# Reordering the first attention layer of a two-layer attention and experts kernel: scores, values and bias in a new order on four engines

## What is computed

```python
x = x + window_attention(group_norm(x))   # layer 0: 8x8 windows, shifted by 4; 12 heads of 8; cosine scores
t = t + local_attention(layer_norm(t))    # layer 1: 6 heads of 16, causal, window of 16
t = t + experts(layer_norm(t))            # 4 experts, best 2, hidden 384
```

```python
qkv = xw @ qkv_w.T + qb                                   # xw: 64 windows of 64 tokens
qn = q / max(norm(q), 1e-12);  kn = k / max(norm(k), 1e-12)
attn = einsum('whid,whjd->whij', qn, kn) * scale + bias + mask
out = einsum('whij,whjd->whid', softmax(attn), v)
out = out @ proj_w.T + proj_b
```

## Time and profile before

| | |
|---|---|
| median of three runs | 470.01 us (470.0 to 472.74) |
| profiled execution | 472.79 us, its span 471.0 us |
| PE busy | 420.6 us (89%) |
| DVE busy | 337.6 us (72%) |
| ACT busy | 342.5 us (73%) |
| POOL busy | 125.2 us (27%) |
| layer 0, steps 0 to 31 | about 28 to 187 us of the span |

### The profile page before, as it was taken

The page is one execution under the profiler, slowest core; times in us unless marked ns, Lnnn a source line. Parts: engine busy times, 40 slices in busy tenths (PEclk is TensorE's granted clock), DMA queues, the critical chain, the costliest instruction groups (busy, mean ns, idle before and its releaser), DMA issues.

```text
span 471.0 us, 14649 instructions
## 1 busy us (share of the span) xinstructions
PE 420.6 (89%) x5292; PEld 318.7 (68%) x5292; DVE 337.6 (72%) x949; ACT 342.5 (73%) x918; POOL 125.2 (27%) x300
## 2 busy tenths in 40 slices
PE   4669999999999987799999998879999999999995
PEld 2436667676766666577777776658865777777773
DVE  4857878878787886667677667463669677777776
ACT  3457887878787873788888887654786777777773
POOL 5122233242424330433343433546502000000000
PEclk9999899999999999999999999876999999999999
DMA  7400000000000000000000000005000503302200
GB/s 206 121 2 1 2 2 0 0 0 0 0 0 0 0 3 1 2 3 2 0 0 0 0 0 3 2 1 135 1 2 22 150 1 83 86 1 83 83 17 17
DMA packets 7861, 12.17 MB, mean 26 GB/s; under 512 B 2179, under 2 KB 6681, under 8 KB 7062
## 3 DMA queue, kind: packets, MB, share of 16 engines
q1 hardware_dynamic: 7322, 11.60, 9.1%
q0 software_dynamic: 96, 0.09, 0.2%
q10 hardware_dynamic: 412, 0.08, 0.1%
HBM read 10.08 MB, written 1.68 MB: 25 GB/s over the span
## 4 chain that ended last, share of the span: by engine, by line
PE 56%; ACT 19%; DVE 15%; issue 6%; DMA 2%; POOL 1%; DVEq 0%; ACTq 0%; POOLq 0%
PE bank L717 7%; PE score_banks L773 5%; PE score_banks L1372 4%; ACT qT L851 4%; PE score_banks L1369 4%; PE score_banks L1370 4%; ACT kT L852 4%; PE bank L705 3%; PE bank L763 3%; PE score_banks L1358 3%; PE score_banks L1359 3%; PE score_banks L1360 3%; ACT probsT L871 3%; DVE qk L959 2%; ACT probsT L868 2%
## 5 line engine op out<-in xcount | busy, mean ns | idle before, releaser
L1521 DVE TENSOR_TENSOR hidden_lo<-hidden,hidden_hi 128x512 fp32r<-128x512 f32 x96 | 65.6, 685 | 22.9 <-ACT hidden_hi L1425 22.8
L1037 POOL TENSOR_TENSOR stack<-qk,ones 128x192 f16<-128x192 f32 x64 | 32.4, 507 | 169.4 <-DVE qk L959 102.4
L894 DVE TENSOR_REDUCE negmax<-score_banks 128x12 bf16<-128x768 f32 (+1 forms) x64 | 48.4, 756 | 25.1 <-PE score_banks L679 25.0
L1423 ACT ACTIVATE hidden<-score_banks 128x512 f32<-128x512 f32 x64 | 38.4, 600 | 26.1 <-PE score_banks L1360 22.1
L705 PEld LDWEIGHTS bank<-vals,probsT 128*64 128x64 f32 (+1 forms) x1536 | 35.4, 124 | 28.9 <-ACT probsT L868 16.2
L705 PE MATMUL bank<-vals,probsT 128*64 128x18 f32 (+1 forms) x1536 | 41.1, 206 | 14.1 <-DVE oT L931 5.0
L717 PE MATMUL bank<-w_qkv,xnT 128*128 128x192 f32 x128 | 39.5, 392 | 7.8 <-DVE qk L959 5.6
L773 PE MATMUL score_banks<-perm,probs 128*128 128x128 f32 x288 | 43.7, 281 | 0.6 <-ACT probs L841 0.6
L1372 PE MATMUL score_banks<-hidden_lo,w_hi 128*96 128x512 f32 x96 | 39.1, 407 | 2.3 <-DVE hidden_lo L1521 2.1
L1369 PE MATMUL score_banks<-hidden_hi,w_hi 128*96 128x512 f32 x96 | 39.0, 406 | 0.6 <-ACT hidden_hi L1425 0.6
L1370 PE MATMUL score_banks<-hidden_hi,w_lo 128*96 128x512 f32 x96 | 38.3, 399 | 0.0
(11 more groups left out here) (189 smaller groups left out, 1038.1 us busy)
## 6 DMA issues: line engine op xcount, KB each, us to landing
xT_all<-gate_scratch SPq DMA_DIRECT2D x8, 768.0 KB, 5.3
x_all<-in_x SPq DMA_DIRECT2D x4, 384.0 KB, 8.3
out<-moe_final SPq DMA_DIRECT2D x8, 192.0 KB, 2.0
w<-in_w SPq DMA_DIRECT2D x1, 579.0 KB
w<-in_w SPq DMA_DIRECT2D x1, 576.0 KB, 5.3
w_qkv<-in_w_qkv SPq DMA_DIRECT2D x2, 144.0 KB, 6.8
perm<-in_permutations SPq DMA_DIRECT2D x1, 256.0 KB, 2.8
bias_f<-col_scratch SPq DMA_DIRECT2D x8, 24.0 KB
```

The costliest lines, as they stand in the source:

```text
L894: v.tensor_reduce(negmax[:].rearrange("p (g h) -> p g h", g=2), score_banks[k][:, :, 0:half].rearrange("p g (h j) -> p g h j", j=KEYS), AX ...
L1423: nc.scalar.activation(hidden[m % 2][:], h_bank[m % HBUF], ACT.Gelu)
L1521: v.tensor_tensor(hidden_lo[m % HBUF][:], hidden[m % 2][:], hidden_hi[m % HBUF][:], ALU.subtract).then_inc(q["hidden_lo"], 1)
```

## The change

It reorders the lists of layer 0; no operation is added or taken away.

- TensorE, step n: first half of the scores, value projection of unit n+1, second half, query and key projection, transposes of the probabilities, output projection or output transposes, stack transposes, subtraction of the maximum, the bias of unit n+1 (`pe_bias`, which waits for both copies of the probabilities that lay in these banks), value product. The bias of unit 0 is laid before step 0.
- ScalarE: squares, probability copy, guess of the root, stack copies, value copies, exponential, key stack.
- VectorE: the bound (L942) comes right behind the sum of squares, ahead of the probability copy.

```diff
     def pe_step(pe, b, k, odd):
         n = 2 * b + k
-        ahead_x = xnT[:, (1 - odd) * T:(2 - odd) * T] if first else xnT
-        pe_scores(pe, n, b, k, ahead_x)
         if first:
-            if not on(n):
-                pe_project_qk(pe, n, b, k, ahead_x)
+            ahead_x = xnT[:, (1 - odd) * T:(2 - odd) * T]
+            slot_v = odd if k == 0 else 1 - odd
+            pe_first_row_groups(pe, n, k)
+            pe_project_v(pe, n + 1, 1 - k, xnT[:, slot_v * T:(slot_v + 1) * T])
+            pe_second_row_groups(pe, n, k)
+            pe_project_qk(pe, n, b, k, ahead_x)
+            pe_probs_transpose(pe, n - 1, 1 - k)
             if k == 0:
                 pe_output_project(pe, n - 1, b - 1)
             else:
                 pe_output_transpose(pe, n - 1, b)
-            pe_probs_transpose(pe, n - 1, 1 - k)
             pe_stacks(pe, n, k)
-            slot_v = odd if k == 0 else 1 - odd
-            pe_project_v(pe, n + 1, 1 - k, xnT[:, slot_v * T:(slot_v + 1) * T])
             pe_shift(pe, n, k)
+            if on(n):
+                pe_bias(pe, n + 1, 1 - k)
             pe_values(pe, n, b, k, odd)
             return
```

```diff
+    def pe_bias(pe, n, k):
+        if on(n):
+            at_least(pe, q["probsT_copied_a"], n - 1)
+            at_least(pe, q["probsT_copied_b"], n - 1)
+            for g2 in range(2):
+                pe.matmul(score_banks[k][:, g2, 0:half], s["twice_ident"][:],
+                          s["bias_h"][:, g2 * half:(g2 + 1) * half], start=True, stop=False, skip_group_check=True)
...
+    def pe_first_row_groups(pe, n, k):
+        if on(n):
+            at_least(pe, q["qkT_ready"], n + 1)
+            pe_products(pe, k, (0, 2)).then_inc(q["row_group_done"], 1)
+
+    def pe_second_row_groups(pe, n, k):
+        if on(n):
+            at_least(pe, q["row_group_done"], n + 1)
+            pe_products(pe, k, (1, 3)).then_inc(q["scores_ready"], 1)
```

```diff
             act_squares(act, n)
             act_copy_probs(act, n - 1, 1 - k)
+            act_norm_guess(act, n)
             act_transposed_stacks(act, n, k)
-            act_norm_guess(act, n)
+            act_values(act, n, k, odd)
             act_exp(act, n, k)
-            act_values(act, n, k, odd)
             act_stacks(act, n, k)
...
             dve_sum_squares(v, n)
+            dve_bound_squares(v, n)
             if on(n - 1):
                 at_least(v, q["probsT_ready"], n)
...
             if k == 0:
                 dve_residual(v, n - 1, b - 1)
-                dve_bound_squares(v, n)
                 dve_statistics(v, n, b)
             else:
                 dve_output(v, n - 1, b)
-                dve_bound_squares(v, n)
```

More of the change, by code:

```diff
@@ L647, in pe_stacks @@
             last.then_inc(q["stackT_ready"], 1)
-    def pe_scores(pe, n, b, k, x):
-        S = score_banks[k]
-        if on(n):
-            if not first and k == 0 and on(n + 2):
+    def pe_bias(pe, n, k):
[5 more added lines that the diff above has]
+                          s["bias_h"][:, g2 * half:(g2 + 1) * half], start=True, stop=False, skip_group_check=True)
@@ new lines, in pe_mask, with pe_products @@
+    def pe_mask(pe, k):
+        for g2 in range(2):
+            Sg = score_banks[k][:, g2, 0:half]
+            pe.matmul(Sg.rearrange("p (t j) -> p t j", t=TILES3), ident_bf[:],
+                      s["band"][:, k, None, :].to_broadcast([P, TILES3, KEYS]),
+                      start=True, stop=False, skip_group_check=True)
+    def pe_products(pe, k, together):
+        S = score_banks[k]
+        for t in range(TILES3):
+            for g in together:
+                g2 = g // 2 if first else g
+                rows = slice(slot * g, slot * (g + 1))
+                at = (t * 2 + g % 2) * KEYS if first else t * KEYS
+                for w in range(P // qrows):
+                    k0 = w * KEYS if first else k * P + w * QBLOCK
+                    last = pe.matmul(S[w * qrows:(w + 1) * qrows, g2, at:at + KEYS],
+                                     qT[rows, t, w * qrows:(w + 1) * qrows], kT[rows, t, k0:k0 + KEYS],
+                                     start=False, stop=True, skip_group_check=True)
+        return last
@@ L654, in pe_scores @@
+    def pe_first_row_groups(pe, n, k):
+        if on(n):
+            at_least(pe, q["qkT_ready"], n + 1)
[4 more added lines that the diff above has]
+            pe_products(pe, k, (1, 3)).then_inc(q["scores_ready"], 1)
+    def pe_scores(pe, n, b, k):
+        if on(n):
+            if k == 0 and on(n + 2):
                 at_least(pe, q["xnT_ready"], b + 2)
@@ L656, in pe_scores @@
             at_least(pe, q["qkT_ready"], n + 1)
[L659 to L683, removed]
@@ L684, in pe_scores @@
-            last.then_inc(q["scores_ready"], 1)
+            pe_mask(pe, k)
+            pe_products(pe, k, (0, 1)).then_inc(q["scores_ready"], 1)
     def buffer_of(k, odd, ahead):
@@ L786, in pe_step @@
                 pe_output_transpose(pe, n - 1, b)
-            pe_probs_transpose(pe, n - 1, 1 - k)
             pe_stacks(pe, n, k)
-            slot_v = odd if k == 0 else 1 - odd
-            pe_project_v(pe, n + 1, 1 - k, xnT[:, slot_v * T:(slot_v + 1) * T])
             pe_shift(pe, n, k)
+            if on(n):
+                pe_bias(pe, n + 1, 1 - k)
             pe_values(pe, n, b, k, odd)
             return
+        pe_scores(pe, n, b, k)
         pe_values(pe, n, b, k, odd)
@@ L1045, in pool_step @@
                                     ALU.subtract).then_inc(q["stack_ready"], 1)
-    return {"pe": pe_step, "pe_values": pe_values, "pe_output_transpose": pe_output_transpose,
+    return {"pe": pe_step, "pe_bias": pe_bias, "pe_values": pe_values, "pe_output_transpose": pe_output_transpose,
             "pe_output_project": pe_output_project, "act": act_step, "dve": dve_step, "pool": pool_step, "normalise": normalise, "q": q}
@@ L1208, in _ @@
             pe.wait_ge(s["bias_split"], 1)
+            a0["pe_bias"](pe, 0, 0)
             steps(pe, a0["pe"], 0, 4)
```

## The result

The changed kernel takes 494.1 us (median of four executions, 488.1 to 498.31) against 470.0 us (467.11 to 472.74): ratio 1.043, 95% interval 1.03 to 1.0561. The profiled execution took 492.28 us, its span 490.4 us, 19.4 more than the span before. It is slower, as forecast, but by 4.3% (24 us by the medians) where 1.7% (8 us) was forecast, and outside the range of 471.5 to 485.

What follows compares the result with a forecast made beforehand. A chain through several engines, no full engine, was taken to bound the kernel. The new loop's 0.27 us over 22 steps (+5.9), +1.5 at the start and +0.5 at the end gave 470.0 + 7.9 = 477.9, rounded 478; range 471.5 to 485.

Steps and rivals of the forecast that it cites:

- The loop: Layer 0: value product, value copies, value projection, second half, rest of TensorE's step; mean 5.04 us a step against 4.775.
- the sign: Whole kernel: slower, 478 us against a median of 470.0; slower by over 1% given 0.73.
- The sum: Steps 5 to 26: twelve terms giving 5.08 us in even steps, 5.00 in odd ones with the bias wait.
- term 4: TensorE's value projection, followed by a change of shape: taken as 0.37 us, from 0.33 up to 0.39.
- the wait of the bias: Odd steps, TensorE: the moved bias waits for VectorE's half of the probability copy, 0.10 to 0.20 us, taken as 0.15.
- the releases: Value product's end to first copy, 0.10 us; copies' end to TensorE's value projection, 0.05 us.
- the subtraction of the maximum: TensorE, between stack transposes and bias: two matmuls of the bias's shape, 0.33 us.
- the clock: TensorE's clock falls in the steady stretch: chance 0.08, about ten stretches, +9 us on top, 487 us.
- The ends: Steps 0 to 4: +1.5 us (0 to +3); steps 27 to 31 and passage to layer 1: +0.5 (-1 to +2).
- The rule on idle gaps: TensorE: by the skill page the new order costs the clock nothing, since its gaps are below 1 us.
- The copies don't decide: Rival, chance 0.12: value product ends before the stack copies, steps take 4.32 us, whole kernel 458 us.
- The loop is shorter: Rival, chance 0.13: several terms and the bias wait together 0.15 us smaller, ends cost nothing, 473 us.

Runs made afterwards that it cites:

- the fillers: Changed kernel plus 12 unread matmuls per step on TensorE, between first half of the scores and value projection: 482.57 us; with 4 instead: 482.81 us.
- the two moves: Changed kernel with value projection back behind stack transposes (490.6 us), exponential back ahead of value copies (486.82 us), or both (460.85 us).
- a load and a half: Kernel before with two added VectorE operations per step (128 x 448 and 128 x 256 fp32) ahead of the refining of the root: 491.4 us.

## Why the prediction was right and where it was wrong

**The loop and the sign were right.** The loop of value product, value copies, value projection and second half of the scores was walked from rows of the kernel before, and it is what the trace after shows and what the buffers, the fillers and the two moves confirm.

**The sum was 0.10 us a step too small.** 5.08 and 5.00 us were counted, 5.18 and 5.10 measured. In the odd step shown, term 4 (value projection) is 0.39 and not 0.37, the wait of the bias is 0.20 and not 0.15 (131.26 to 131.79 less 0.33), the releases 0.11 and 0.06 for 0.10 and 0.05, and the rest is 0.01 at a time in the read spacings. In the even step before it the largest difference is 0.08: the subtraction of the maximum takes 0.41 up to the bias (126.28 to 126.69) and not 0.33, though the prediction had put no wait of the bias there. Over 22 steps that is 22 x 0.10 = 2.2 us: the loop costs 8.1 us there, 5.9 had been forecast.

**The step that failed is the clock.** The prediction gave it 0.08 and counted no stretch in the forecast. The argument was that TensorE would be busy some 85%, between 72% with a fall and 92% with none, and it stopped there; the share came out at 84% and the clock fell. The price was wrong as well: "up to 0.9 more for one stretch" was the difference of step 4 of the old order to the mean of later steps. The kernel before with four buffers settles it, since its step 4 ran at full clock and took 4.62 us in place of 5.70, so that stretch had cost 1.1 us:

```profile
50.83:55.45 4.62, 4.18 (x71) 3.08 (x71) 3.87 (x14) 4.44 (x14) 0.77 (x3) 1.00 0.01 4
```

In the changed kernel a stretch costs 1.5 us; in the old order with a load and a half it costs 0.83 (120.81 - 11 x (5.20 + 5.48) = 3.3 us over four). That the price follows how much of the loop runs through TensorE, all its matmuls in the changed kernel and few beside VectorE's list with the loads, fits these numbers but was not tested by itself. In the profiled execution the clock accounts for 7.5 us of steps 5 to 26 and for the passage to layer 1 (15.56 us, with the clock at 0.67; 12.67 with 12 fillers and no stretch there). With the 12 fillers, whose profile has no stretch in steps 5 to 26 or the passage, the median is 482.57 us, inside the range of the prediction: it is the clock that carried the result out of it. From the forecast for the profiled execution, 480.7, the differences lead to the measured one: + 2.2 for the longer steps, + 7.5 for the clock in them, + 3.0 for the passage, + 4.0 for the start (5.5 against 1.5), - 0.5 for the end that was forecast, - 4.7 in the unchanged parts: 492.2, measured 492.28. Of the start, 1.5 us lie ahead of the first maximum and no run ties them to the change.

**The ends.** Steps 0 to 4 were put at +1.5 and took +4.0, with two half-clock stretches in them where before had one; with 12 fillers, and no stretch after 36.5 us, they took 27.05 us, +1.0. Steps 27 to 31 and the passage together were put at +0.5 (-1 to +2) and took +3.0: nothing in steps 27 to 30, and all of it in step 31 and the passage, where the clock was at half for 10.2 us.

**The rule on idle gaps.** The Trainium skill, page "TensorE: Matmul & The Clock Gate", section "Why this matters for your kernels", asks for no long idle gap between bursts. The longest gap in a steady step here is 0.81 us and the clock fell five times. By that rule the kernel would have come out near the 480.7 of the forecast; the measurement decides, and in this kernel it says that keeping to the rule was not enough.

**The rivals.** "The copies don't decide" is excluded by the trace, but its sum, 4.32 us a step, came close for the kernel in which they really don't (4.32 and 4.36 with four buffers). That is partly luck: the rival's route runs from the end of the stack transposes to their copies, but in the odd step shown the transposes end at 111.07 and the copies start at 111.36, behind ScalarE's guess, which the route leaves out. "The loop is shorter" was wrong in direction. The chance of the clock was too small for an effect that one known stretch of the kernel before had shown after 72% busy.

## What to carry to other kernels

When an operation is moved ahead in a hand-written pipeline, list what its own waits ask for, in units of steps: here a copy that overwrites one of two buffers asked for the last operation of the same step, which was free as long as it stood late. A move that brings such a consumer forward needs more buffers with it; four turned 494 us into 459 (three were not tried). And when a change adds idle time to TensorE, price the clock as a term of its own: look up in the trace what TensorE did where the clock held and where it fell, and take the price of a stretch from a step that ran at both clocks. Here the prices were 0.83 to 1.5 us for 3.4 us at half clock.

## What the runs showed of the hardware

TensorE's clock fell from 2.4 to 1.2 GHz (1.00 to 0.50) in steady steps in which TensorE was idle for no more than 0.81 us at once, for 3.4 us each time. In the old order with a load and a half it did so too, with waits of about 0.9 us. The number of falls differs between executions of one kernel: the changed kernel's mean clocks were 0.941 to 0.958 in four executions and its times 488.1 to 498.31 us. A stretch of 3.4 us at half clock cost 1.5, 1.1 or 0.83 us in three kernels. And work that nobody needs, put into a wait, made a kernel faster: the 12 fillers, 482.57 against 494.1 us.
